# Mixer A of a hybrid layer: sums over the states taken as fp32 transposes that add up in PSUM, with the gate on the token side

## The reference, cut to what matters

```python
residual = x
xz = _rmsnorm(x, norm_w) @ in_proj_w.T
x_part, z = jnp.split(xz, 2, axis=-1)
u = jax.nn.silu(conv4(x_part) + conv_b)              # depthwise, 4 taps
dt, Bm, Cm = jnp.split(u @ x_proj_w.T, [8, 24], axis=-1)
delta = jax.nn.softplus(dt @ dt_proj_w.T + dt_proj_b)
# per token: h = exp(delta*A)*h + delta*u*B ;  y = sum over 16 states of h*C
y = _selective_scan(u, delta, A, Bm, Cm, D)          # + u*D
out = (y * jax.nn.silu(z)) @ out_proj_w.T + residual
```

## Time and profile before

| what | us |
|---|---|
| median of 3 runs (all three) | 1105.76 (1105.76, 1108.03, 1101.1) |
| span of the profiled execution | 1033.5 |
| PE busy | 963.6 (93%) |
| DVE busy | 741.9 (72%) |
| POOL busy | 601.0 (58%) |
| ACT busy | 575.3 (56%) |

### The profile page before, as it was taken

How to read it: one execution, slowest core, us unless ns; L and a number is a source line. 1 busy time by engine, 2 the same in 40 slices (tenths; PEclk the granted TensorE clock), 3 DMA queues, 4 the chain that set the end, 5 groups by cost and what they waited for, 6 DMA issues and landing times. The chain is left out here.

```text
span 1033.5 us, 16232 instructions
## 1 busy us (share of the span) xinstructions
PE 963.6 (93%) x4715; PEld 683.1 (66%) x4715; DVE 741.9 (72%) x1211; ACT 575.3 (56%) x1109; POOL 601.0 (58%) x467
## 2 busy tenths in 40 slices
PE   6898999988899999999999869988999999999997
PEld 2323333323566899999997436666666899999996
DVE  3989998999488566666666876865588566666665
ACT  6575656665443455555555676765733455555553
POOL 3679797999522888567312648530212888566412
PEclk9999989998999999999999889998999999999999
DMA  4222223243422145220003000000602133322104
GB/s 151 74 71 74 72 82 90 78 105 88 152 66 68 32 113 118 71 79 27 27 14 108 24 0 2 1 1 0 194 24 69 32 89 87 94 64 68 35 14 127
DMA packets 60400, 69.41 MB, mean 67 GB/s; under 512 B 6232, under 2 KB 42848, under 8 KB 60320
## 3 DMA queue, kind: packets, MB, share of 16 engines
q1 hardware_dynamic: 55328, 58.15, 18.8%
q0 software_dynamic: 4992, 10.23, 4.1%
HBM read 57.74 MB, written 10.62 MB: 66 GB/s over the span
## 5 line engine op out<-in xcount | busy, mean ns | idle before, releaser
L795 POOL TENSOR_TENSOR a_hc<-a_h,a_c_sb 128x512 f32<-128x512 f32 x128 | 159.6, 1272 | 29.7 <-DVE a_h L695 26.9
L471 PE MATMUL ps<-a_hc,eye 128*128 128x512 f32 x256 | 135.4, 647 | 10.2 <-POOL a_hc L795 9.5
L610 ACT ACTIVATE ps<-a_delta,a_neg_a 128x512 f32<-128x512 f32 x128 | 87.4, 688 | 69.1 <-DVE a_h L695 67.9
L471 PEld LDWEIGHTS ps<-a_hc,eye 128*128 128x128 f32 x256 | 46.7, 199 | 77.9 <-issue 38.9
L695 DVE TENSOR_TENSOR_SCAN a_h<-ps,a_state,a_b_u 128x512 f32<-128x512 f32 x64 | 78.6, 1264 | 1.0 <-ACT ps L610 0.8
L695 DVE TENSOR_TENSOR_SCAN a_h<-ps,a_b_u 128x512 f32<-128x512 f32 x64 | 75.1, 1205 | 3.9 <-ACT ps L610 3.7
L1183 PE MATMUL ps<-g_ring_rounded,g_q_hi_rounded 128*128 x312 | 77.0, 337 | 0.0
L1183 PE MATMUL ps<-f_ring_rounded,f_q_hi_rounded 128*128 x312 | 77.0, 337 | 0.0
L1049 POOL DMA_INDIRECT token_rows<-f_rows,f_back x39 | 37.9, 971 | 60.1 <-DVE f_rows L1707 45.2
L1049 POOL DMA_INDIRECT token_rows<-g_rows,g_back x39 | 37.8, 969 | 53.9 <-DVE g_rows L1707 32.4
L675 DVE TENSOR_TENSOR a_b_u<-a_du,ps 128x1024 f32<-128x1024 f32 x57 | 68.0, 1193 | 0.9 <-PE ps L458 0.8
(11 more groups left out here) (472 smaller groups left out, 2781.8 us busy)
## 6 DMA issues: line engine op xcount, KB each, us to landing
a_c_sb<-c_rows SPq DMA_DIRECT2D x64, 256.0 KB, 3.3
f_ring<-in_gu SPq DMA_DIRECT2D x16, 469.0 KB, 4.4
g_ring<-in_gu SPq DMA_DIRECT2D x16, 469.0 KB, 4.0
f_ring<-in_dn SPq DMA_DIRECT2D x8, 512.0 KB, 6.0
g_ring<-in_dn SPq DMA_DIRECT2D x8, 512.0 KB, 6.0
xn_rows<-f_work SPq DMA_DIRECT2D x8, 256.0 KB, 4.4
f_rows<-token_rows SPq DMA_DIRECT2D x8, 256.0 KB, 4.9
xn_rows<-g_work SPq DMA_DIRECT2D x8, 256.0 KB, 4.0
```

Of the source, the lines that this page charges most:

```text
L471: nc.tensor.matmul(ps[:, Y + f, :], k.eye[:, :], hc[:, s % WAITING, :], start=False, stop=(n == NST - 1)).then_inc(y_added, 1)
L610: nc.scalar.activation(ps[:, A + m % NA, :], delta[:, f, cols(g)], ACT.Exp, scale=neg_a[:, f, n:n + 1])\
L795: nc.gpsimd.tensor_tensor(hc[:, m % WAITING, :], h[:, s % DEPTH, :], c_sb[:, i % RING, :], ALU.mult)\
```

## The change

y is now gathered token by token (128 tokens on the partitions, channels along the row). Each product `hc` (128 channels x 512 tokens) is added by four transposes of 128x128 that accumulate in the same PSUM bank, instead of one matmul with the identity. For that the skip term is four matmuls per half with u as the stationary side, and z is projected token by token (two matmuls of 128x256 per call). The gate writes a new tile `y_tok`. Because the output projection needs channels on the partitions again, the gated y is turned back: four transposes per half into bank `O` (TURN0, TURN1), each copied by ACT to `yz` (`turned_back`), and only then projected. That puts two more uses of `O` in each chunk, and the other pieces of work move: the positions n and steps s of nearly all uses shift. The add of the projection moves on DVE from n = 4 to n = 5, the low parts of the rows from 7 to 8, and POOL's `delta` and `du` from steps 24 and 26 to 25 and 27. The selector `sel` is half as large.

```diff
             def z_of(c, half, bank):
                 b, t0 = divmod(c * CH, SEQ)
+                for i in range(BLOCKS // 2):
+                    t = PADC + t0 + (half * BLOCKS // 2 + i) * P
+                    last = nc.tensor.matmul(ps[:, bank, i * DI:(i + 1) * DI], xp[:, b, t:t + P], w_in[:, DI:2 * DI],
+                                            start=True, stop=True)
+                return last
+
+            def turn_back(g, f, bank):
+                pe.wait_ge(yz_ready, g * FT + f + 1)
+                for i in range(BLOCKS):
+                    last = nc.tensor.transpose(ps[:, bank, i * P:(i + 1) * P], y_tok[:, f, i * P:(i + 1) * P], k.eye[:, :])
+                return last
...
             def between(g, n):
                 if g + 1 < NCH:
-                    if n in (0, 3):
-                        in_turn(g, TAPS0 + n // 3)
-                    if n in (1, 4):
-                        convolution(g + 1, n // 4, O, TAPS // 2, TAPS).then_inc(o_ready, 1)
-                if g and n == 6:
-                    in_turn(g, PROJECT)
-                if g + 1 == NCH and n in (0, 8, 12):
-                    in_turn(g, {0: CENTRE0, 8: CENTRE1, 12: CENTRE2}[n])
-                if g + 1 == NCH and n in (3, 10, 14):
-                    in_turn(g, {3: VAR0, 10: VAR1, 14: VAR2}[n])
+                    if n in (0, 2):
+                        in_turn(g, TAPS0 + n // 2)
+                    if n in (1, 3):
+                        convolution(g + 1, n // 2, O, TAPS // 2, TAPS).then_inc(o_ready, 1)
+                if g + 1 == NCH and n in (0, 9, 12):
+                    in_turn(g, {0: CENTRE0, 9: CENTRE1, 12: CENTRE2}[n])
+                if g + 1 == NCH and n in (2, 11, 14):
+                    in_turn(g, {2: VAR0, 11: VAR1, 14: VAR2}[n])
+                if g and n in (4, 5, 7):
+                    in_turn(g, {4: TURN0, 5: TURN1, 7: PROJECT}[n])
                 if g + 1 < NCH:
-                    if n == 8:
+                    if n == 9:
                         in_turn(g, XPROJ)
-                    if n in (10, 12):
-                        in_turn(g, DT0 + (n - 10) // 2)
+                    if n in (11, 13):
+                        in_turn(g, DT0 + (n - 11) // 2)
...
-                        nc.tensor.matmul(ps[:, Y + f, :], skip[:, f, :], u[:, f, cols(g)], start=True, stop=False)
+                        for i in range(BLOCKS):
+                            t = g * CH + i * P
+                            nc.tensor.matmul(ps[:, Y + f, i * P:(i + 1) * P], u[:, f, t:t + P], skip[:, f, :],
+                                             start=(i == 0), stop=False, skip_group_check=True)
                     pe.wait_ge(hc_ready, s + 1)
-                    nc.tensor.matmul(ps[:, Y + f, :], k.eye[:, :], hc[:, s % WAITING, :],
-                                     start=False, stop=(n == NST - 1)).then_inc(y_added, 1)
+                    for i in range(BLOCKS):
+                        last = nc.tensor.matmul(ps[:, Y + f, i * P:(i + 1) * P], hc[:, s % WAITING, i * P:(i + 1) * P],
+                                                k.eye[:, :], start=False, stop=(n == NST - 1 and i == BLOCKS - 1),
+                                                is_transpose=True, skip_group_check=True)
+                    last.then_inc(y_added, 1)
...
+            def turned_back(g, f):
+                turn(g, TURN0 + f)
+                nc.scalar.activation(yz[:, f, :], ps[:, O, :], ACT.Copy).then_inc(o_read, 1)
...
+                if g and s in (8, 11):
+                    turned_back(g, s // 11)
...
-                if g and n == 4:
+                if g and n == 5:
                     add(g - 1)
...
-                        if s == 24:
+                        if s == 25:
                             pool.wait_ge(log_done, g + 2)
...
-                        if s == 26:
+                        if s == 27:
                             pool.wait_ge(delta_ready, g + 2)
```

More of the change, by code:

```diff
@@ L328, in mixer_a_stage @@
                 loaded=k.x_loaded)
[L329 to L332 removed]
+    TAPS0, TAPS1, TURN0, TURN1, PROJECT, XPROJ, DT0, DT1, Z0, Z1, CENTRE0, VAR0, CENTRE1, VAR1, CENTRE2, VAR2 = range(16)
+    OUTPUT = [TURN0, TURN1, PROJECT]
+    USES = [[TAPS0, TAPS1, XPROJ, DT0, DT1, Z0, Z1], [TAPS0, TAPS1, *OUTPUT, XPROJ, DT0, DT1, Z0, Z1],
+            [TAPS0, TAPS1, *OUTPUT, XPROJ, DT0, DT1, Z0, Z1], [CENTRE0, VAR0, *OUTPUT, CENTRE1, VAR1, CENTRE2, VAR2],
+            OUTPUT]
+    BLOCKS = CH // P
     def use(g, what):
@@ L375, in convolution, with z_of @@
                 return last
-            def z_of(c, f, bank):
+            def z_of(c, half, bank):
                 b, t0 = divmod(c * CH, SEQ)
-                return nc.tensor.matmul(ps[:, bank, :], w_in[:, DI + f * P:DI + (f + 1) * P],
-                                        xp[:, b, PADC + t0:PADC + t0 + CH], start=True, stop=True)
+                for i in range(BLOCKS // 2):
[8 more added lines that the diff above has]
+                return last
             def u_done(c):
@@ L418, in in_turn @@
                     last = nc.tensor.matmul(ps[:, O, :], k.ones[:, :], delta[:, 0, cols(c)], start=True, stop=True)
+                elif what in (TURN0, TURN1):
+                    last = turn_back(g - 1, what - TURN0, O)
                 elif what == PROJECT:
@@ L585, in between @@
                         parts(c, f, O).then_inc(o_read, 1)
-                    if s == 24:
+                    if s == 25:
                         softplus_exp(c)
-                    if s == 25:
+                    if s == 26:
                         softplus_log(c)
-                    if s in (27, 30):
-                        f = (s - 27) // 3
-                        turn(g, Z0 + f)
-                        nc.scalar.activation(sz[:, f, cols(c)], ps[:, O, :], ACT.Copy).then_inc(o_read, 1)
+                    if s in (28, 30):
+                        half = (s - 28) // 2
+                        turn(g, Z0 + half)
+                        nc.scalar.activation(sz[:, half, cols(c)], ps[:, O, :], ACT.Copy).then_inc(o_read, 1)
             def half_sequence(g):
@@ L642, in _ @@
             finish_norm()
+            turned_back(NCH, 0)
+            turned_back(NCH, 1)
         @block.vector
@@ L700, in between @@
                     gate(g - 1)
-                if g and n == 4:
+                if g and n == 5:
                     add(g - 1)
-                if g + 1 < NCH and n == 7:
+                if g + 1 < NCH and n == 8:
                     low_rows(g + 1, O).then_inc(o_read, 1)
```

41 lines of the change are left out of this document (21 added, 20 removed).

## The result

The changed kernel took 1114.59 us (median of four, 1113.12 to 1115.96) against 1104.54 for the kernel before in runs on the same chip: a ratio of 1.0090 [1.0062, 1.0118], 10 us slower. The forecast was 1109, its range 1100 to 1121, and slower by over 1% had 0.18. The time lies in the range and under the 1%, if barely. It lies outside the forecast's own 1105 to 1113, though, and the loss is 10 us where the sum gave 3.1: the sign is right, the size is a third, and the wide range covers the miss. Of the steps, some came out to the tenth and two were badly undersized.

The account below looks back on a forecast made before the run. DVE was taken to bound the kernel, with PE's relief mostly idle time. Terms -2.1 - 1.8 + 2.75 + 0.05 + 1.0 + 3.2 = +3.1 us on about 1105.8 gave 1109, range 1100 to 1121.

Parts of the forecast that it names:

- DVE as the bound, PE's relief mostly idle time: Mixer A: DVE sets the pace; a faster PE can give back only some 8 us inside the steps.
- Chunk 0: DVE's 2.67 us wait around ACT's Silu block falls to 0.6 with the half convolution at n = 2: -2.1 us.
- `du`: POOL makes it one product later, so DVE stalls 1.7, 0.35 and 0.7 us in chunks 0 to 2: +2.75 us.
- A product's price: On PE, four transposes cost 0.44 us per product instead of 0.94, saving 64 us over 128 products.
- the rival of the dear product: Transposes' weight loads don't overlap, so four take 1.1 us and PE keeps its load: about 1110 us, chance 0.05.
- The skip term: On PE, 16 records per chunk instead of four, taken as 3.5 us against 1.9 before.
- Gates: DVE's waits for PE's last products at the ends of chunks 0 and 1 shrink from 3.0 to about 1.2: -1.8 us.
- ACT's copies and the moved add, about 0: Chunks 1 to 3: a 0.35 us stall in chunk 1, 0.3 less in chunk 2, 0 in chunk 3: +0.05 us.
- The end: End of mixer A: turning back and copies before the last projection put the last add at 271.9: +1.0 us, before clock effects.
- The head of the next stage: First matmuls after mixer A, a round of norm matmuls, run at 1.2 GHz: some +1.2 us.
- The clock: PE falls to 1.2 GHz at mixer A's end: projection +1.6, turning back +0.4, next stage's first matmuls +1.2: +3.2 us.
- the rival through most of a chunk: PE stays at 1.2 GHz through most of each chunk, delaying adds, gates and end by 14 to 15 us: 1120, chance 0.22.

Follow-up runs that it names:

- the second profile of before: The kernel before, unchanged, run and profiled once more; ratio 1.0011, 230.8 us from mixer A's first scan to its last add.
- the old places: The changed kernel with its transposes, but the other pieces of work set back to the positions of the kernel before; ratio 1.0022 to the kernel before.
- extra transposes: The changed kernel with four more transposes of a constant ahead of each broadcast of a row B; ratio 1.0115 to the kernel before.
- the kernel with sums first: The changed kernel, but at n = 2 PE adds the chunk's last two products before the half convolution; ratio 1.0088 to the kernel before.
- the moved places alone: The kernel before, with its plain matmul products and gate, but the changed kernel's positions for the other work; ratio 1.0111 to the kernel before.
- broadcasts three times: The changed kernel with each broadcast of a row B computed three times into its bank; ratio 1.0189 to the kernel before.
- the last kernel: The changed kernel with positions of the kernel before, two free banks at the end and transposes of ones behind the last six products; ratio 0.9977 to the kernel before.

## Why the prediction was right, and where it was not

**DVE as the bound, PE's relief mostly idle time: right.** PE gave up 44 us of product time, and even in its best arrangement the stage is only 2 to 5 us shorter.

**Chunk 0: right in what stays, not shown in what it is worth.** The stall of 2.67 should become 0.6; it is 0.59. But 2.67 goes with a fall of the clock that the second profile of before doesn't have (1.16 there), so the gain is 0.6 to 2.1 us, and the old places reach 0.60 without the moved convolution.

**`du`: right in size, wrong in what it is worth.** 1.7, 0.35 and 0.7 were walked; 1.70, under 0.3 and 0.69 came. But put back, the gates took nearly all of it. The sum treated it as additive.

**A product's price: right at the full clock when eight transposes stand together** (1.04 us); the rival of the dear product fell. The group costs 91.1 us, not 60, and the low clock is the smaller part of that: with extra transposes, at 0.87 to 0.95, it still costs 80.2. The rest is that many products wait for POOL and stand alone: four transposes by themselves take 0.60 to 0.66 us, not 0.44, since the last one's 0.27 is paid each time.

```profile
L490 PE MATMUL ps<-eye,a_hc 128*128 128x128 f32 x512 | 80.2, 296 | 22.6 <-POOL a_hc L829 21.9
```

The skip term was 9.1 us for four chunks, 2.3 each, for 3.5.

**Gates: the step that failed first.** "Now the wait shrinks, from 3.0 to about 1.2": it is 2.04 and 0.48, and 1.52 at the gate of chunk 2, 4.0 in all. At chunk 0 the step fails by its own numbers. DVE came to this gate at 99.01 - 1.71 = 97.3; with -2.1 from chunk 0 and +1.7 from `du` it comes at 96.9, to products walked to 99.1, so the wait had to grow to 2.2, and 2.04 was measured. The 2.1 of chunk 0 was counted as a gain although PE at the gate takes it back. The walk priced the half convolution ahead of the last two products at 1.9 us. It took 3.57, and the kernel with sums first shows that the gate waited for it. The gate of chunk 2 has no term in the sum: there a sum of the next norm, moved from n = 3 to n = 2, stands ahead of the last products (2.08 us at the low clock, and the products 1.91 after it). Moving the half convolution is harmful at the full clock too, as the moved places alone show.

**"ACT's copies and the moved add, about 0": the step that failed worst.** 4.0 us of waits inside the stage, 3.1 more than before. The hole behind the Silu block did stay as it was (0.89 and 0.99 before, 1.80 now, at 174 us), but the add no longer stands in it and waits 1.68 of its own at 179. I looked at the copy's 0.6 us on ACT and not at the chain through it: products, turning back, copy behind the Silu block, second turning back, projection at 3.45, add. The add had been moved one step; it wanted two.

**The end: close in sum, by errors that cancel.** +4.2 was forecast, 1.2 of it in the next stage; +3.9 was measured up to the add alone. From the end of POOL's last product to the add: 4.05 us before, 279.38 - (267.71 + 3.73) = 7.94 after, +3.9 where +1.0 + 1.6 + 0.4 = 3.0 was forecast for this stretch. The projection took 3.39 for 1.96 (+1.4, forecast 1.6), turning back 1.06 and 1.11 for 0.6 each (+1.0, forecast 0.4), and the chain through two copies the rest. The head of the next stage was to lose 1.2 to the clock. Its first record lost nothing: it lasts 1.10 us and starts 1.0 after the add in both. But the head did lose time, in another way. From the last add to the first product of the expert loop it is 70.3 us, against 68.4 and 68.8 in the two profiles of before, and 1.3 of it lies in one operation of DVE, 13 us behind the add (before, then after, with POOL's beside it):

```profile
282.62 0.72 DVE L1478 TENSOR_TENSOR f_x_lo<-xn,f_x_hi 128x512 fp32r<-128x512 f32 x1
282.75 4.65 POOL L1022 TENSOR_TENSOR f_ring_rounded<-f_ring,f_ring_rounded 128x1876 fp32r<-128x1876 f32 x1
```

```profile
291.95 4.19 POOL L1054 TENSOR_TENSOR f_ring_rounded<-f_ring,f_ring_rounded 128x1876 fp32r<-128x1876 f32 x1
292.38 4.30 DVE L1510 TENSOR_TENSOR f_x_lo<-xn,f_x_hi 128x512 fp32r<-128x512 f32 x1
```

In the three profiles without transposes of products (the two of before, the moved places) DVE started it first and it took 0.68 to 0.97 us. In the eleven with them POOL started first, DVE's took 2.6 to 4.6 us, and the products of the expert loop began 69.8 to 70.7 us behind the add. Even the best arrangements here pay this 1 to 2 us.

**The clock.** The forecast had it low only at the end, the rival through most of a chunk: 14 to 15 us, adds 5, gates 6, end 3.2. Measured 0.77 to 0.88, adds 3.1 more, gates 1.0 more, end 3.9. What happened lies between the two, nearer to the rival than its chance of 0.22 said. And neither had it whole: at the same low clock the old places cost nothing inside the steps. It takes a low clock (or dense PE work) *and* work put where the slack was.

## What to carry to other kernels

A cheaper instruction on an engine that isn't the bound frees time, but the places in which other work was put belonged to the old durations; try the cheap instruction with every place kept first, and move one thing at a time after. Walk each moved step at both clocks when the change itself empties PE, and follow a new hand-over (PE to ACT to PE) to who waits at its end, not only to its own length. When one wait is walked to the tenth, ask what stands 1 us behind it: here the mended wait for `du` came back at the gates.

## What was new about the hardware

- The granted clock doesn't follow PE's busy time alone: with broadcasts three times PE was busy for 66.4 of 69 us in the first stretch and had 0.82; with extra transposes 61.7 and 0.95. The fillers that failed use 64 rows of weights in fp32r, those that worked 128 rows in fp32; which of the two matters wasn't tried.
- Fp32 transposes of constants raised the clock as plain matmuls of the same operands did (0.95, 0.94, 0.91 in both), and it stayed at 1.00 from 254 to 262 us of the last kernel, with PE doing nothing but transposes to 261.
- Thirteen us behind mixer A, a TENSOR_TENSOR of DVE (`f_x_lo`, 128x512, in SBUF) looks as if it waited for one of POOL: it took 0.68 to 0.97 us when it started 0.02 to 0.4 us before POOL's, and 2.6 to 4.6 when it started during it. In all eleven such profiles it ended 0.5 to 0.6 us behind the end of POOL's (292.38 + 4.30 = 296.68 and 291.95 + 4.19 = 296.14 in after).
- Two executions of the same program differed by 35 to 40 us in each expert loop (202.4 and 236.9), with the timed runs all near 1105: one profile's span can be far from the median, and where it differs should be looked up before anything is put "around" it.
